# Last layer of a two-layer transformer kernel: top values turned before the first base products, next group's masks made in tile 5, base tile 0 opened with its x products

## The chip, the cores and the metric

The kernel runs on one core of a Trainium2 chip. The metric is the device time of one execution in microseconds (us), the median of several runs. Five engines work side by side, each with its own instruction queue, and meet only at semaphores: TensorE (PE, matrix products into PSUM; its weight loads are shown as PEld), VectorE (DVE), ScalarE (ACT), GpSimd (POOL) and SyncE (SP), which issues the DMAs here.

## The reference, cut to what matters

```python
x = x + tanh(g_xattn[0]) * L0_xattn(layernorm(x), ...)   # long convolution
x = x + tanh(g_ffn[0])   * L0_ffn(layernorm(x), ...)     # 8 experts and a shared one
x = x + tanh(g_xattn[1]) * L1_xattn(layernorm(x), ctx)   # attention, 16 heads
x = x + tanh(g_ffn[1])   * L1_ffn(layernorm(x), ...)     # the layer that is changed

# L1_ffn; B = 16 sequences, S = 128, D = 256, H = 704, 8 experts, rank 16
gate_logits = x @ gate_w.T
topw, sel = top_k(gate_logits, 2)
topw = softmax(topw, axis=1)              # over the sequence, not over the two
base_up, base_gate = x @ w_up.T, x @ w_gate.T
for e in range(8):
    c = sum(where(sel == e, topw, 0))
    lo_up   = 2 * (x @ up_A[e].T   @ up_B[e].T)
    lo_gate = 2 * (x @ gate_A[e].T @ gate_B[e].T)
    h_e = silu(base_up + lo_up) * (base_gate + lo_gate)
    ch = c * h_e
    mixed_h += ch
    lora_down += 2 * (ch @ down_A[e].T @ down_B[e].T)
out = mixed_h @ w_down.T + lora_down
```

## The kernel before

Four stages follow each other (convolution, experts, attention, and the last layer, about 620 to 894 us). Each takes the 16 sequences in G = 4 groups of 4 (512 tokens). The last layer works transposed: hidden units on partitions, the 512 tokens of a group along the free axis. The 704 hidden units are 6 tiles (j = 0 to 5, the last with 64 rows). Every product is done as three products of high and low halves (`three`, L1625, L1630), which ACT (high half, a copy) and DVE (low half, a subtraction) make for every operand.

Each token uses two experts. For its first expert a tile is computed as base products (`d_base`): 12 products of x with the weights (6 for up, 6 for gate), and 6 of the masked adapter values z. For its second, `d_delta` adds the difference of the adapters on top of the same PSUM bank (6 products). After each, ACT applies SiLU (L733) and DVE multiplies (L1202, L1206; after the second also the sum, L1210). ACT and DVE then split the two results (L741, L747; L1216, L1222) and `d_down` multiplies them down. `(j, 0)` is a tile's first expert and `(j, 1)` its second. TensorE runs base of tile j, delta of tile j-1, down of tile j-2.

At a change of group TensorE computes the adapter values of the next group (`d_adapters_in`, 12 products, into the PSUM areas U_[0] and G_[0]), then `d_down` of tiles 4 and 5, then `d_base(g+1, 0)`. DVE multiplies the adapter values with the masks (`d_split_z`, L1190, four of them, counted by `zm_ready`), ACT copies the high halves (L725), DVE makes the low halves (L1193, counted by `zL_ready`). Only when L1190 has read U_[0] and G_[0] may tile 0 be written there. DVE goes on with `d_mix` (L1228 to L1238) of the group that ends, and only then with the next group's first tile.

The masks come from the router: eleven small DVE steps find the two best experts (`top2_step`), TensorE turns the values to rows (`d_turn_tops`, L1653), DVE and ACT take the softmax over the sequence, SP stores the 16 rows and loads them back spread over all partitions (L387, L391, into `rb`), DVE compares them with each partition's expert number (`masks`, L1175, two instructions) and POOL subtracts the two masks (L488, `dMD`). `masks(n)` waits for the load; `d_split_z` waits for POOL.

The order on every engine is the order in which this code is written; nothing reorders it. `Steps.take(n)` weaves small steps between larger ones.

Of the kernel before, what the change touches and what calls it, by code (L numbers as in the profile page):

```python
# [107 lines left out]
def flamingo_kernel(nc, x, ctx_nat, ctx_half, ctx_t, ctx_one, filt, bias, gates, w0, wr, w1, gw, ramp_in, out):  # L108
    es = ExitStack()
    with es:  # L110
# [135 lines left out]
        for j in range(1, SJ):  # L246
# [40 lines left out]
        d_logits, lg_taken, tops_ready, tops_turned, tops_taken, topmax_ready, cexp_ready = (  # L287
            sem("d_logits"), sem("lg_taken"), sem("tops_ready"), sem("tops_turned"), sem("tops_taken"),
            sem("topmax_ready"), sem("cexp_ready"))
        rows_ready, rows_stored, rows_loaded = sem("rows_ready"), sem("rows_stored"), sem("rows_loaded")  # L290
        dM_ready, dMD_ready = sem("dM_ready"), sem("dMD_ready")
        z_psum, zm_ready, zH_ready, zL_ready = sem("z_psum"), sem("zm_ready"), sem("zH_ready"), sem("zL_ready")
        ev_ready, dsilu_ready, dscaled_ready, ch_ready, sum_ready = (
            sem("ev_ready"), sem("dsilu_ready"), sem("dscaled_ready"), sem("ch_ready"), sem("sum_ready"))
# [500 lines left out]
        def _(dve):  # L795
# [293 lines left out]
            def d_norm(lo, hi):  # L1089

                return norm_steps(hi - lo, lambda b: X[:, lo + b], pstat[:, lo:hi], pmv[:, lo:hi], pvar[:, lo:hi],
                                  ptmp[:, lo:hi], prs[:, lo:hi], pnb[:, lo:hi], None)
# [57 lines left out]
            def group_top2(n):  # L1150
                return Steps(lambda i: top2_step(i, n), N_TOP2)

            def rows_taken(n):

                dve.wait_ge(tops_turned, n + 1)
                if n:
                    dve.wait_ge(rows_stored, 16 * n)
                t_psum = TQ[0:4 * BG, P:2 * P] if n == 0 else U_[0][0:4 * BG, 0:P]
                nc.vector.tensor_copy(prow, t_psum).then_inc(tops_taken, 1)
# [6 lines left out]
            def rows_scale(n):  # L1166
                dve.wait_ge(cexp_ready, n + 1)
                link(nc.vector.reciprocal(mrcp, msum))
                nc.vector.tensor_scalar(prow[0:2 * BG], prow[0:2 * BG], mrcp, None, ALU.mult).then_inc(rows_ready, 1)

            def masks(n):

                dve.wait_ge(rows_loaded, 16 * (n + 1))
                for r in (2, 3):
                    nc.vector.tensor_scalar(rb[n % 2][:, r], rb[n % 2][:, r], expert_col, LORA_ALPHA,  # L1175
                                            ALU.is_equal, ALU.mult).then_inc(dM_ready, 1)

            def d_low_x(g):
                for k in range(DT):
                    dve.wait_ge(xH_ready, 2 * (G + g) + k + 1)  # L1180
                    nc.vector.tensor_tensor(xL[:, k], pxT[:, k], xH[:, k].bitcast(F32), ALU.subtract
                                            ).then_inc(xL_ready, 1)
# [13 lines left out]
            def d_rows(g, j, k):  # L1196

                i = at_ev[j, k]
                pr = TAIL if j == SJ - 1 else P
                dst = (dc1, dc2)[k]  # L1200
                dve.wait_ge(ev_ready, NE * g + i + 1)
                nc.vector.tensor_tensor(dscaled[0:pr, i % 2], G_[j % 2][0:pr], rb[g % 2][0:pr, k], ALU.mult  # L1202
                                        ).then_inc(dscaled_ready, 1)
                dve.wait_ge(dsilu_ready, NE * g + i + 1)
                dve.wait_ge(dscaled_ready, NE * g + i + 1)
                nc.vector.tensor_tensor(dst[0:pr, j % 2], dscaled[0:pr, i % 2], dsilu[0:pr, i % 2], ALU.mult  # L1206
                                        ).then_inc(ch_ready, 1)
                if k == 1:
                    dve.wait_ge(ch_ready, 1 + NE * g + i + 1)
                    nc.vector.tensor_tensor(dc2[0:pr, j % 2], dc2[0:pr, j % 2], dc1[0:pr, j % 2], ALU.add  # L1210
                                            ).then_inc(sum_ready, 1)

            def d_low_first(g, j):
                pr = TAIL if j == SJ - 1 else P
                dve.wait_ge(cH_ready, SJ * g + j + 1)
                nc.vector.tensor_tensor(dcL[0:pr, j % 2], dc1[0:pr, j % 2], dcH[0:pr, j % 2].bitcast(F32),  # L1216
                                        ALU.subtract).then_inc(cL_ready, 1)
# [40 lines left out]
            def d_tiles(g, more, top2):  # L1258
                norm = d_norm(B - BG, B) if g == 0 else Steps()
                for j in range(2, SJ):  # L1260
                    d_rows(g, j, 0)
                    top2.take(4)
                    if more and j == 4:
                        rows_scale(g + 1)
                    if more and j == 5:
                        norm.take_all()
                    d_rows(g, j - 1, 1)
                    top2.take_all()
                    if more and j == 3:
                        rows_taken(g + 1)  # L1270
                    if more and j == SJ - 1:
                        d_low_x(g + 1)
                    d_low_first(g, j)
                    if more and j == 3:
                        rows_shift(g + 1)
                    d_low_sum(g, j - 1)
                    if j >= 3:
                        norm.take(8)
                d_rows(g, SJ - 1, 1)
                d_low_sum(g, SJ - 1)  # L1280
                if more:
                    masks(g + 1)
                    dve.wait_ge(dn_ready, 1 + g)
                    d_split_z(g + 1)
                    dve.wait_ge(zL_ready, 4 * (g + 2))
                d_mix(g)
                top2 = group_top2(g + 2) if g + 2 < G else Steps()
                if more:
                    d_first(g + 1, top2)
                d_finish(g)  # L1290
                return top2
# [81 lines left out]
        def _(pe):  # L1373
# [273 lines left out]
            def d_turn_tops(n):  # L1647

                pe.wait_ge(tops_ready, n + 1)
                if n:  # L1650
                    pe.wait_ge(dsilu_ready, NE * (n - 1) + at_ev[2, 1] + 1)
                t_psum = TQ[0:4 * BG, P:2 * P] if n == 0 else U_[0][0:4 * BG, 0:P]
                nc.tensor.transpose(t_psum, ptop, ident[:]).then_inc(tops_turned, 1)  # L1653

            def d_adapters_in(g):

                pe.wait_ge(xL_ready, 2 * (G + g + 1))
                for r, dst in enumerate((U_[0], G_[0])):
                    a = [((w1H[:, r * D + k * P:r * D + (k + 1) * P], w1L[:, r * D + k * P:r * D + (k + 1) * P]),
                          (xH[:, k], xL[:, k])) for k in range(DT)]  # L1660
                    three(dst, a).then_inc(z_psum, 1)

            def d_base_in(g, j, part):

                pr = TAIL if j == SJ - 1 else P
                for at, dst, zr_ in ((0, U_[j % 2], 0), (2 * P, G_[j % 2], 2)):
                    if j >= 2 and zr_ == 2:
                        pe.wait_ge(dscaled_ready, NE * g + at_ev[j - 2, 1] + 1)
                    a = [(tuple(w[:, 0:pr] for w in w1_tile(j, at + k * P, P)), (xH[:, k], xL[:, k]))
                         for k in range(DT)]  # L1670
                    lora = [(tuple(w[:, 0:pr] for w in w1_tile(j, 4 * P + at // 2, P)), (dzH[:, zr_], dzL[:, zr_]))]
                    if part == "all":
                        mm = three(dst[0:pr], a + lora, skip=True)
                    elif part == "x":
                        mm = three(dst[0:pr], a, stop=False, skip=True)
                    else:
                        mm = three(dst[0:pr], lora, start=False, skip=True)
                return mm

            def d_base(g, j, part="all"):  # L1680
                if j >= 2:
                    pe.wait_ge(dsilu_ready, NE * g + at_ev[j - 2, 1] + 1)
                else:
                    pe.wait_ge(zm_ready, 4 * (g + 1))
                if j == 4 and g + 1 < G:
                    pe.wait_ge(tops_taken, g + 2)
                if j == 0:
                    pe.wait_ge(zL_ready, 4 * g + 2)
                d_base_in(g, j, part).then_inc(ev_ready, 1)

            def d_delta(g, j):

# [88 lines left out]
            pe.wait_ge(w1L_ready, W1K)  # L1781
            pe.wait_ge(shifted, 8 * G)
            d_adapters_in(0)
            d_base_in(0, 1, "x")
            pe.wait_ge(lg_taken, 1)
            d_turn_tops(0)
            d_turn(1)
            d_router(1)
            d_base(0, 0)
            d_base(0, 1, "z")  # L1790
            d_delta(0, 0)
            for g in range(G):
                d_tiles(g, g + 1 < G)
# [66 lines left out]
```

## Time and profile before

| | us |
|---|---|
| median of 3 runs | 894.28 |
| lowest, highest | 894.27, 897.79 |
| the profiled execution, its own time | 895.68 |
| its span, first to last instruction | 894.0 |
| PE busy | 794.3 (89%) |
| DVE busy | 611.6 (68%) |
| ACT busy | 325.1 (36%) |
| POOL busy | 164.1 (18%) |
| mean granted TensorE clock | 0.962 of full |

The page divides the span into 40 slices of 22.35 us; each digit is the busy share in tenths. The last layer is the last 12 slices:

```
PE   2887879699999999999998999987599999899995
DVE  5899999654466465457545888896368766677754
PEclk9999999899999999999999999978799999999997
```

TensorE is at nine tenths in most of it. The exceptions are the layer's opening (slices 28 and 29) and the end. PEclk is the clock granted to TensorE, in tenths of full speed; a 9 is full. It has two levels, 2.4 GHz (1.00) and 1.2 GHz (0.50). Times within the span are counted from its start, and all durations come from this one execution.

### The profile page before, as it was taken

To read this page: it belongs to the slowest core of one execution; us is meant where nothing else is said; L and a number is where in the kernel's file an instruction comes from. 1 tells how busy PE (TensorE), PEld (TensorE's weight loads), DVE (VectorE), ACT (ScalarE), POOL (GpSimd) and SP (SyncE) were. 2 spreads that over 40 slices of the span, in tenths; PEclk is the share of its full clock that TensorE was granted. 3 is DMA by queue.
4 is the path that set the end of the run, shared out by engine and by line. 5 is a ranking of instruction groups with operands and counts; after the bars stand their busy time and mean duration, and the time that the engine had idled before them with its cause. 6 is when DMAs were issued, how large, how long until landed. Compare 5 with 4: busy or idle time off the path is not lost. (4 is left out here: it accounts for less than half of the span.)

```text
span 894.0 us, 13688 instructions
## 1 busy us (share of the span) xinstructions
PE 794.3 (89%) x4708; PEld 638.3 (71%) x4708; DVE 611.6 (68%) x1231; ACT 325.1 (36%) x521; POOL 164.1 (18%) x176
## 2 busy tenths in 40 slices
PE   2887879699999999999998999987599999899995
PEld 2565657588878888888885666655477788787884
DVE  5899999654465466457545888896368766677754
ACT  2120212133433242342233677856235235343221
POOL 1899999500000000000000010100000000000000
PEclk9999999899999999999999999978799999999997
DMA  7221212000000000001001112110101001001000
GB/s 271 72 86 50 70 47 65 18 1 1 1 0 0 0 0 0 0 0 33 18 1 44 48 55 84 53 41 1 48 0 48 1 25 48 1 25 48 24 0 25
DMA packets 21147, 30.24 MB, mean 34 GB/s; under 512 B 3760, under 2 KB 16112, under 8 KB 20464
## 3 DMA queue, kind: packets, MB, share of 16 engines
q1 hardware_dynamic: 21104, 29.69, 10.1%
q8 instruction: 24, 0.39, 0.2%
q14 instruction: 19, 0.16, 0.1%
HBM read 27.55 MB, written 2.13 MB: 33 GB/s over the span
## 5 line engine op out<-in xcount | busy, mean ns | idle before, releaser
L1630 PE MATMUL bank<-R 128*128 128x512 f32 (+4 forms) x1104 | 230.9, 371 | 26.5 <-DVE R L1193 15.2
L1630 PEld LDWEIGHTS bank<-R 128*128 128x128 f32 (+2 forms) x1104 | 186.6, 191 | 68.3 <-issue 19.3
L1484 PE MATMUL bank<-R 128*128 128x512 f32 (+1 forms) x816 | 198.0, 392 | 1.9 <-issue 1.9
L1484 PEld LDWEIGHTS bank<-R 128*128 128x128 f32 (+1 forms) x816 | 146.7, 185 | 33.1 <-issue 2.2
L1009 DVE TENSOR_TENSOR A<-bank,A 128x512 f32<-128x512 f32 (+1 forms) x68 | 47.0, 692 | 119.9 <-PE bank L1484 119.9
L1497 PEld LDWEIGHTS bank<-R 128*128 128x128 f32 (+1 forms) x816 | 105.8, 190 | 10.8 <-issue 4.0
L1497 PE MATMUL bank<-R 128*128 128x256 f32 (+1 forms) x816 | 109.4, 284 | 2.5 <-DVE R L1020 2.1
L574 ACT ACTIVATE A<-bank 128x512 f32<-128x512 f32 (+1 forms) x68 | 40.6, 597 | 194.7 <-PE bank L1484 194.7
L1409 PE MATMUL bank<-A 128*128 128x256 f32 x128 | 44.1, 427 | 28.2 <-DVE A L857 19.2
L449 POOL TENSOR_TENSOR A<-A 128x256 f32<-128x256 f32 x64 | 64.2, 1002 | 10.6 <-DVE A L868 10.6
L1202 DVE TENSOR_TENSOR A<-bank,A 128x512 f32<-128x512 f32 (+1 forms) x48 | 32.9, 685 | 38.4 <-PE bank L1630 38.1
L857 DVE TENSOR_TENSOR A<-A 128x512 f32<-128x512 f32 x64 | 55.0, 861 | 0.4 <-ACT A L514 0.4
L1409 PEld LDWEIGHTS bank<-A 128*128 128x128 f32 x128 | 20.9, 196 | 47.4 <-DVE A L857 27.8
L478 POOL TENSOR_TENSOR R<-A,R 128x960 f32 x8 | 17.8, 2224 | 195.5 <-ACT R L627 195.5
L733 ACT ACTIVATE A<-bank 128x512 f32<-128x512 f32 (+1 forms) x48 | 28.6, 597 | 66.2 <-PE bank L1630 66.0
L1551 PE MATMUL bank<-ident,A 128*128 128x128 f32 x256 | 38.9, 301 | 13.7 <-ACT A L632 13.3
L868 DVE TENSOR_TENSOR A<-bank,A 128x512 f32<-128x512 f32 x64 | 43.5, 680 | 8.8 <-PE bank L1411 7.4
L1014 DVE TENSOR_TENSOR A<-A 128x512 f32<-128x512 f32 (+1 forms) x68 | 46.8, 688 | 3.1
L1551 PEld LDWEIGHTS bank<-ident,A 128*128 128x128 f32 x256 | 31.3, 154 | 23.8 <-ACT A L632 17.8
L1062 DVE TENSOR_REDUCE small<-bank 128x8 f32<-128x1024 f32 x32 | 39.0, 1220 | 13.3 <-PE bank L1541 13.1
L1020 DVE TENSOR_TENSOR R<-A,R 128x512 fp32r<-128x512 f32 (+1 forms) x68 | 46.2, 680 | 1.3 <-ACT R L583 1.2
L472 POOL MEMSET A<- 128x512 f32 x4 | 1.9, 524 | 229.3 <-DVE A L1014 229.3
(166 smaller groups left out, 1098.1 us busy)
## 6 DMA issues: line engine op xcount, KB each, us to landing
A<-in_w SPq DMA_DIRECT2D x17, 384.0 KB, 3.1
A<-rows_d SPq DMA_DIRECT2D x4, 1024.0 KB, 4.6
A<-in_w SPq DMA_DIRECT2D x8, 480.0 KB, 3.6
A<-in_ctx_one SPq DMA_DIRECT2D x8, 272.0 KB, 3.6
A<-in_ctx_half SPq DMA_DIRECT2D x8, 256.0 KB, 3.1
A<-in_ctx_nat SPq DMA_DIRECT2D x4, 512.0 KB, 3.6
A<-in_ctx_t SPq DMA_DIRECT2D x128, 16.0 KB, 2.0
out<-X SPq DMA_DIRECT2D x4, 512.0 KB, 2.9
```

The lines of the kernel that those rows point to most:

```text
L449: nc.gpsimd.tensor_tensor(zh[:, u], zr[:, u, :, 0:HALF, :], zr[:, u, :, HALF:, :], ALU.add).then_inc(zh_ready, 1)
L574: nc.scalar.activation(b_silu[0:pr, j % 2], G_[j % 2][0:pr], ACT.Silu).then_inc(silu_ready, 1)
L857: nc.vector.tensor_tensor(kv[:, u], vT[:, :, t0:t0 + I0].unsqueeze(3).to_broadcast([P, 8, I0, I0]), c.unsqueeze(2).to_broadcast([P, 8, I0, ...
L868: nc.vector.tensor_tensor(zr[:, u], yb[u].rearrange("p (q i j) -> p q i j", q=8, i=I0), c.unsqueeze(3).to_broadcast([P, 8, I0, I0]), ALU.m ...
L1009: nc.vector.tensor_tensor(b_scaled[0:pr, j % 2], U_[j % 2][0:pr], b_comb[0:pr, 0 if j < EJ else 1], ALU.mult).then_inc(scaled_ready, 1)
L1014: nc.vector.tensor_tensor(b_h[0:pr, j % 2], b_silu[0:pr, j % 2], b_scaled[0:pr, j % 2], ALU.mult).then_inc(h_ready, 1)
L1020: nc.vector.tensor_tensor(hL[0:pr, j % 2], b_h[0:pr, j % 2], hH[0:pr, j % 2].bitcast(F32), ALU.subtract).then_inc(hL_ready, 1)
L1409: nc.tensor.matmul(y[:, 0:n], diag, kv0, start=True, stop=False, skip_group_check=True)
L1484: mm = nc.tensor.matmul(dst[0:pr], wX[:, j, at + k * P:at + k * P + pr], mX[:, k], start=(n == 0), stop=(n == 5))
L1497: mm = nc.tensor.matmul(DN[:, b * D:(b + 1) * D], hX[0:pr, j % 2, b * P:(b + 1) * P], wX[0:pr, j, 4 * P:], start=(j == 0 and n == 0 and b ...
L1551: mm = nc.tensor.transpose(PTP[:, h * P:(h + 1) * P], E_[:, k % 2, h], ident[:])
L1630: mm = nc.tensor.matmul(dst, a, m, start=start and n == 0, stop=stop and n == len(prods) - 1, skip_group_check=skip)
```

## The change

There are three edits, all in the last layer.

1. On TensorE, `d_turn_tops(0)` moves ahead of the x products of tile 1 (`d_base_in(0, 1, "x")`) in the layer's opening.
2. On DVE, `masks(g + 1)` moves from behind tile 5 of group g into tile 5: behind the products of (5, 0), ahead of those of (4, 1). POOL's subtraction follows the masks by semaphore and so moves with them.
3. On TensorE, `d_base` of tile 0 waits for `zm_ready` only, issues its 12 x products, and waits for `zL_ready` ahead of the 6 z products. Before, both waits stood ahead of all 18.

```diff
@@ DVE, d_tiles
                     if more and j == 5:
                         norm.take_all()
+                        masks(g + 1)
                     d_rows(g, j - 1, 1)
@@
                 d_low_sum(g, SJ - 1)
                 if more:
-                    masks(g + 1)
                     dve.wait_ge(dn_ready, 1 + g)
                     d_split_z(g + 1)
@@ PE, d_turn_tops
                     pe.wait_ge(dsilu_ready, NE * (n - 1) + at_ev[2, 1] + 1)
+                else:
+                    pe.wait_ge(lg_taken, 1)
@@ PE, d_base
-            def d_base(g, j, part="all"):
+            def d_base(g, j):
@@
                 if j == 0:
+                    d_base_in(g, j, "x")
                     pe.wait_ge(zL_ready, 4 * g + 2)
-                d_base_in(g, j, part).then_inc(ev_ready, 1)
+                    d_base_in(g, j, "z").then_inc(ev_ready, 1)
+                else:
+                    d_base_in(g, j, "all").then_inc(ev_ready, 1)
@@ PE, the opening
             d_adapters_in(0)
+            d_turn_tops(0)
             d_base_in(0, 1, "x")
-            pe.wait_ge(lg_taken, 1)
-            d_turn_tops(0)
             d_turn(1)
             d_router(1)
             d_base(0, 0)
-            d_base(0, 1, "z")
+            pe.wait_ge(zL_ready, 2)
+            d_base_in(0, 1, "z").then_inc(ev_ready, 1)
```

The order on TensorE in the layer's opening, with what each instruction waits for (L1653 of before is L1655 of the change; L1598 turns the next group's x, L1643 is the router):

```order
 L1630 MATMUL bank<-R 128x512 [waits xL_ready,shifted,w1L_ready]
-L1630 MATMUL bank<-R 128x512 x23
-L1653 MATMUL bank<-ident,A 16x128 [waits tops_ready,lg_taken]
+L1630 MATMUL bank<-R 128x512 x11
+L1655 MATMUL bank<-ident,A 16x128 [waits lg_taken,tops_ready]
+L1630 MATMUL bank<-R 128x512 x12
 L1598 MATMUL bank<-ident,A 128x128 [waits vN_ready]
 L1598 MATMUL bank<-ident,A 128x128 x7
 L1643 MATMUL bank<-gw_sb,A 128x8 [waits xT_ready]
 L1643 MATMUL bank<-gw_sb,A 128x8 x7
-L1630 MATMUL bank<-R 128x512 [waits zL_ready,zm_ready]
-L1630 MATMUL bank<-R 128x512 x17
```

The turn stands behind 12 products in place of 24, and ahead of the 12 that were in front of it.

The order on DVE around the end of tile 5 of the first group (the same at the other two changes of group):

```order
+L1175 TENSOR_SCALAR A<-A,small 128x512 x2
 L1202 TENSOR_TENSOR A<-bank,A 128x512
 L1206 TENSOR_TENSOR A<-A 128x512
@@ -773,5 +774,4 @@
 L1210 TENSOR_TENSOR A<-A 64x512
 L1222 TENSOR_TENSOR R<-A,R 64x512
-L1175 TENSOR_SCALAR A<-A,small 128x512 x2
 L1190 TENSOR_TENSOR A<-bank,A 128x512 x4
 L1193 TENSOR_TENSOR R<-A,R 128x512 x4
```

The two mask instructions leave the place ahead of L1190 and stand ahead of (4, 1)'s L1202. Behind them are now that tile's L1202, L1206 and L1210, the next group's L1181, and the rest of tile 5.

The order on TensorE at the change to the second group:

```order
 L1630 MATMUL bank<-R 128x256 x12
-L1630 MATMUL bank<-R 128x512 [waits zL_ready,zm_ready]
-L1630 MATMUL bank<-R 128x512 x17
+L1630 MATMUL bank<-R 128x512 [waits zm_ready]
+L1630 MATMUL bank<-R 128x512 x11
+L1630 MATMUL bank<-R 128x512 [waits zL_ready]
+L1630 MATMUL bank<-R 128x512 x5
 L1598 MATMUL bank<-ident,A 128x128 [waits w_mixed,vN_ready]
```

Twelve of the 18 products of tile 0 no longer stand behind the wait for `zL_ready`.

## Rows read from the trace of the kernel before

**Rows 1.** The waits of TensorE: engine, line waited for, us, times, longest.

```profile
PE bank L1630 <- DVE R L1193: 15.2, 4, 9.6
```

**Rows 2.** Timeline, the layer's opening: start, us, instruction, [idle before it and its releaser].

```profile
624.84 7.25 PE L1630 MATMUL bank<-R 128*128 128x512 f32 x24 [1.87 <-DVE R L1181]
626.40 0.19 DVE L1148 TENSOR_REDUCE A<-A 128x4 f32<-128x32 f32 x1
...
631.92 0.27 PE L1653 MATMUL bank<-ident,A 128*16 128x128 f32 x1
...
640.03 0.88 DVE L1175 TENSOR_SCALAR A<-A,small 128x512 f32<-128x512 f32 x2 [5.96 <-DMA A<-rows_d]
...
642.29 2.49 DVE L1190 TENSOR_TENSOR A<-bank,A 128x512 f32<-128x512 f32 x4 [1.38 <-POOL A L488]
...
646.12 9.86 PE L1630 MATMUL bank<-R 128*128 128x512 f32 x30 [9.63 <-DVE R L1193]
```

**Rows 3.** Timeline, the second change of group (groups 1 to 2).

```profile
750.06 0.68 DVE L1202 TENSOR_TENSOR A<-bank,A 128x512 f32<-128x512 f32 x1
...
758.25 0.87 DVE L1175 TENSOR_SCALAR A<-A,small 128x512 f32<-128x512 f32 x2
759.20 1.27 POOL L488 TENSOR_TENSOR A<-A 128x512 f32<-128x512 f32 x1 [60.01 <-DVE A L1175]
760.56 2.48 DVE L1190 TENSOR_TENSOR A<-bank,A 128x512 f32<-128x512 f32 x4 [1.44 <-issue]
...
764.39 5.92 PE L1630 MATMUL bank<-R 128*128 128x512 f32 x18 [1.69 <-DVE R L1193]
765.49 0.69 DVE L1228 TENSOR_TENSOR A<-bank,A 128x512 f32<-128x512 f32 x1
...
770.36 0.69 DVE L1202 TENSOR_TENSOR A<-bank,A 128x512 f32<-128x512 f32 x1
...
770.95 4.34 PE L1630 MATMUL bank<-R 128*128 128x512 f32 x18
...
772.42 1.01 ACT L707 ACTIVATE A<-bank 128x1024 f32<-128x1024 f32 x1
```

**Rows 4.** Timeline, the first change of group.

```profile
692.11 8.80 PE L1630 MATMUL bank<-R 128*128 128x512 f32 x48 [0.50 <-DVE R L1181]
...
703.11 5.96 PE L1630 MATMUL bank<-R 128*128 128x512 f32 x18 [2.20 <-DVE R L1193]
```

**Rows 5.** Timeline, the third change of group.

```profile
813.43 1.29 DVE L1181 TENSOR_TENSOR R<-A,R 128x512 fp32r<-128x512 f32 x2
...
815.45 0.59 ACT L733 ACTIVATE A<-bank 64x512 f32<-64x512 f32 x1 [0.16 <-PE bank L1630]
...
825.65 12.87 PE L1630 MATMUL bank<-R 128*128 128x512 f32 x54 [1.71 <-DVE R L1193]
```

**Rows 6.** Stretches of TensorE: from:to, us, busy (x), granted clock, DMA share, GB/s.

```profile
634.00:635.00 1.00, 0.46 (x4) 1.00 0.01 3
...
652.00:652.50 0.50, 0.50 (x4) 0.98 0.00 0
...
703.00:703.50 0.50, 0.39 (x1) 0.72 0.00 0
...
706.50:707.00 0.50, 0.50 (x3) 0.87 0.00 0
```

**Rows 7.** The load of the spread rows: the second group change's issue, and all four loads' landing.

```profile
745.82 0.32 SPq L391 DMA_DIRECT2D A<-rows_d  x1
...
DMA to landing us min/median/max: 4.3/4.6/4.8
```

**Rows 8.** Timeline of DVE and POOL in the first stage.

```profile
153.97 0.72 POOL L449 TENSOR_TENSOR A<-A 128x256 f32<-128x256 f32 x1
154.09 0.65 DVE L943 TENSOR_TENSOR small<-small,ramp 128x32 f32<-128x32 f32 x1
...
161.22 0.19 DVE L943 TENSOR_TENSOR small<-small,ramp 128x32 f32<-128x32 f32 x1
```

## The prediction, made before the changed kernel ran

> **What bounds the kernel now.** I read the busy table first: TensorE is busy 89% of the span, so what its queue waits for is the candidate. In the view of waits, one row of the last layer stands out: the products of L1630 wait 15.2 us in four waits for L1193, the low halves of z [rows 1]. The timeline shows the four: 9.63 us at the opening [rows 2], 2.20, 1.69 and 1.71 us at the three changes of group [rows 3 to 5]. The wait is not the whole price. The 18 products behind the wait at 764.39 take 5.92 us, the 18 at 770.95 take 4.34 us [rows 3]. The granted clock says why: 1.00 until the restart at 703.11, half speed (1.2 GHz) from about then, full again (2.4 GHz) from about 706.6 [rows 4, 6]. So a change of group costs its wait and 5.92 - 4.34 = 1.6 us of slow products. Inside the groups TensorE hardly waits; whatever is saved at these four places moves all that follows.
>
> **Edit 1, the turn.** At 624.84 TensorE starts 24 products and only then turns the top values, at 631.92 [rows 2]. The values were ready at 626.6 (626.40 + 0.19), so the turn waits for its place in the queue alone. It now stands 12 products earlier. A product at full clock takes (4.34 - 0.39)/17 = 0.23 us, with 0.39 us as the part of a product that overlaps nothing (an estimate: the 4.34 us row holds 18 of them); those skipped run behind the clock's rise. The turn comes 12 x 0.23 = 2.8 us earlier, at about 629.1, still behind 626.6. From there the chain is a pure one: softmax, store, load, masks, POOL, L1190. DVE stands idle 5.96 us before the masks for the load alone, and 1.38 us for POOL [rows 2]. The whole chain moves by 2.8 us, and the displaced products fill time in which TensorE would idle anyway.
>
> **Edit 3 at the opening.** TensorE restarts at 646.12, when the second L1193 is done. L1190 ended at 642.29 + 2.49 = 644.78 [rows 2]. With x first it restarts 1.3 us sooner, and its 12 x products outlast the making of the low halves. Together 2.8 + 1.3 = 4.1 us. One cost is unknown: after this restart the clock stays low until 652.0 (5.9 us), while at 703.11 it stays low for 3.5 us [rows 6]. If the low clock lasts 3.5 us in the new opening it gains 1.2 us more (half of 2.4); if it lasts 3.5 us longer than before it gains 1.7 less. I take it unchanged.
>
> **Edit 2, the masks.** It takes three things out of DVE's path to L1190 and puts two into tile 5. Before, from the masks' start to L1190's is 760.56 - 758.25 = 2.31 us [rows 3]: masks, POOL, hand-over. In tile 5 the masks cost 0.87 us. Behind them on DVE are L1202, L1206 and L1210 of (4, 1), then L1181, for which the next group's adapter products wait.
>
> The second cost is POOL. Its 1.27 us subtraction used to run while DVE waited; now it runs beside DVE. In the first stage, a small DVE operation with both inputs in SBUF takes 0.65 us when it is issued under a POOL operation, and 0.19 us alone; it ends just when POOL does (154.74 against 154.69) [rows 8]. L1202 has one input in PSUM and I take it as free; L1206 has both in SBUF, would start 0.7 us behind the masks, and POOL ends 1.35 us behind them: 0.6 us more. So DVE is 0.87 + 0.6 = 1.47 us late from L1206 on. The bounds are 0.87 (POOL hinders nothing) and 0.87 + 1.27 = 2.1 us (POOL holds up L1202 too).
>
> The Trainium skill, "SBUF — State Buffer", section "Who interferes with whom", says the same in general: a VectorE instruction with two SBUF inputs contends with a GpSimd instruction that reads SBUF, one with a single SBUF input does not, and the loser blocks fully. By it the sum is the one I take; a reader of the removed wait alone, without it, would forecast 1.8 us more over three groups.
>
> What DVE's lateness costs TensorE depends on the slack of L1181. At the first change there is none: the adapter products already waited 0.50 us for it [rows 4], so TensorE gets the full 1.47 us and its wait becomes 1.97 us. At the third, L1181 ends at 814.72 and the products before the adapters end at about 815.3 (the ACT row at 815.45, less a product's overlap) [rows 5]: slack 0.55, cost 0.9 us. The second looks the same.
>
> Then the gain. DVE reaches L1190 2.31 - 1.47 = 0.84 us earlier than before, at 759.7, ends it at 762.2; TensorE ended its down products at 764.39 - 1.69 = 762.70 and will now at 763.6. So there is no wait in front of tile 0 any more. The second L1193 follows L1190's end by 1.3 us (763.5): the split of tile 0 is hardly needed here, edit 2 alone nearly does it. A queue that runs on also loses the overlap of about 0.2 us that a stop exposes. Per change of group: wait removed, plus 0.2, plus 1.6 of clock, less the lateness:
> - first: 2.20 + 0.2 + 1.6 - 1.47 = 2.5 us
> - second: 1.69 + 0.2 + 1.6 - 0.9 = 2.6 us
> - third: 1.71 + 0.2 + 1.6 - 0.9 = 2.6 us
>
> **What is late next.** The router of group g + 2 waits for L707, which hangs on DVE's chain: it ended at 773.43 [rows 3] and gains only the 0.84 us of DVE, to 772.6. TensorE would come to it at 775.3 - 2.6 = 772.7. So the second change keeps 2.5 us, the first about the same. DVE's mixing (L1228 from 765.49 to the next L1202 at 770.36) [rows 3] also gains only 0.84 us, and tile 0's products will be ready some 1.8 us ahead of it; the 18 products of tile 1 cover that.
>
> The clock is the other thing. At the first change the adapters' wait becomes 1.97 us. Waits of 2.20, 1.69 and 1.71 us were each followed by the low clock; the stretch with the router's 1.48 us wait kept 1.00 [rows 6]. 1.97 is on the wrong side: I count 1.6 us against it and keep 0.9 us there. At the other two the wait is 0.9 us, on the right side.
>
> The load must have landed when DVE reaches the masks. At the second change it is issued at 745.82 and lands 4.3 to 4.8 us later, 750.1 to 750.6, while DVE is there at 750.06 [rows 3, 7]: 0 to 0.5 us of wait, mostly within the slack; I take 0. At the other changes the store before the load was quicker.
>
> **Sum.** 4.1 + 0.9 + 2.5 + 2.6 = 10.1 us. The profiled execution took 895.68 us, of which 894.0 are its span; it becomes 885.6. It lies 1.40 us above the median, so the median goes from 894.28 to 884.2 us.
>
> **Rivals.**
> - *POOL hinders nothing and the clock holds.* Then DVE is late by 0.87 us only, each change keeps 0.6 us more, and the first loses nothing to the clock: 4.1 + 3.1 + 3.1 + 3.2 = 13.5, giving 880.8 us. For it: L1202's class of operation is unhindered. Against: rows 8. Chance 0.15.
> - *The adapters' wait brings the low clock at every change.* Three waits of 0.9 to 2.0 us, each followed by 1.6 us of slow products: 4.1 + 0.9 + 0.9 + 1.0 = 6.9, giving 887.4 us. Against: 1.48 us did nothing. Chance 0.13.
> - *DVE's mixing takes the wait's place.* If tile 0's late start on DVE and ACT is not covered by tile 1, each change gives what DVE's chain gains, 0.84 us: 4.1 + 2.5 = 6.6, giving 887.7 us. For it: DVE was just in time before. Chance 0.13.
> - *It gives nothing at the changes and little at the opening*, because the chain behind the turn is not what ends the wait: within 0.5% of before. Against: the load as releaser in rows 2. Chance 0.05.
> - *Slower: the masks block DVE for a load that lands late.* In tile 5 everything that feeds TensorE is queued behind them. A load that is L us late makes TensorE L us later at each change and brings the clock's 1.6 us with it; without both, the gains add up to 4.1 + 2.5 + 2.6 + 2.6 = 11.8 us. It decides where 3 x (L + 1.6) is more than 11.8, from L = 2.3 us. With L = 5, a load of twice its length, 19.8 - 11.8 = 8.0 us slower, 902.3 us. Four loads land within 0.5 us of each other. Chance 0.02.
>
> The forecast itself has 0.52.
>
> **Range.** It reaches from 880.4, just past the rival at 880.8, to 888.2, past those at 887.4 and 887.7. Outside are the last two rivals (0.07), and of the others what the opening's -1.2 to +1.7 us carries over the ends, about 0.13. No-change is about 0.5% here, 4.5 us, so faster means below 889.8: chances 0.93 faster, 0.05 the same, 0.02 slower.
>
> **What the changed profile would show.** The turn near 629, the masks near 637.3, the restart of TensorE near 642. L1175 directly behind (5, 0)'s L1206, with POOL's L488 beside L1202, and the L1206 behind it near 1.3 us in place of 0.69. No wait for L1193 or L1190 at the changes of group and full clock in tile 0; a wait of 2.0 us for L1181 at the first change with half clock behind it, and of about 0.9 us at the others. I am wrong if waits appear before tile 2 of the new groups, if L1175 waits for the DMA, or if L1206 keeps 0.69 us.

## The result and the profile after

| | before | changed |
|---|---|---|
| median, us (4 runs each) | 895.03 | 884.62 |
| lowest, highest | 894.27, 897.79 | 884.33, 886.95 |
| ratio, 95% interval | | 0.988 (0.986 to 0.989) |
| profiled execution, its span | 895.68, 894.0 | 884.61, 882.9 |

The change is 1.2% faster, 10.4 us by the medians. The forecast was 884.2 us, with a range of 880.4 to 888.2; it was counted from 894.28 us, the median of the three runs then on record.

Of TensorE's waits in the last layer, L1193's 15.2 us [rows 1] are gone. The longest waits of these products (L1630) in the changed kernel:

```profile
PE bank L1630 <- DVE A L1190: 5.0, 1, 5.0
PE bank L1630 <- DVE R L1238: 4.9, 1, 4.9
PE bank L1630 <- DVE R L1181: 4.4, 3, 1.9
```

The wait for L1190 is what is left of the opening's 9.63 us. The one for L1238, at the end, was there before with the same 4.9 us. Of the three for L1181, the opening's 1.86 us is old too; those at the changes of group, 1.82 and 0.76 us, stand in place of 0.50 and none.

To see where the time went, the layer is cut at rows that both kernels have: the first L1181 (low half of x), and for each group the L1202 of (5, 0), the first of the group's with 64 rows (the mark, below). The end of the last piece is that of the last L1244, the final sum (890.60 us before, 879.53 after). Before:

```profile
623.40 1.28 DVE L1181 TENSOR_TENSOR R<-A,R 128x512 fp32r<-128x512 f32 x2
...
686.11 0.68 DVE L1202 TENSOR_TENSOR A<-bank,A 64x512 f32<-64x512 f32 x1 [0.62 <-PE bank L1630]
...
748.66 0.68 DVE L1202 TENSOR_TENSOR A<-bank,A 64x512 f32<-64x512 f32 x1 [2.12 <-PE bank L1630]
```

After:

```profile
624.48 1.28 DVE L1181 TENSOR_TENSOR R<-A,R 128x512 fp32r<-128x512 f32 x2
...
682.15 0.68 DVE L1202 TENSOR_TENSOR A<-bank,A 64x512 f32<-64x512 f32 x1 [0.62 <-PE bank L1630]
...
742.18 0.68 DVE L1202 TENSOR_TENSOR A<-bank,A 64x512 f32<-64x512 f32 x1 [2.12 <-PE bank L1630]
...
801.15 0.68 DVE L1202 TENSOR_TENSOR A<-bank,A 64x512 f32<-64x512 f32 x1 [2.12 <-PE bank L1630]
```

The opening, 686.11 - 623.40 = 62.71 us, became 57.67; the first change of group, 748.66 - 686.11 = 62.55, became 60.03. The same differences for every kernel of this study, each from its own profile:

| us | opening | change 1 | change 2 | change 3 | end | sum |
|---|---|---|---|---|---|---|
| before | 62.71 | 62.55 | 61.25 | 58.51 | 22.18 | 267.20 |
| the change | 57.67 | 60.03 | 58.97 | 56.20 | 22.18 | 255.05 |
| the change, again | 57.84 | 60.07 | 59.03 | 56.20 | 22.17 | 255.31 |
| edit 1 alone | 60.11 | 62.50 | 61.28 | 58.49 | 22.18 | 264.56 |
| edit 2 alone | 62.85 | 60.03 | 59.38 | 56.20 | 22.18 | 260.64 |
| edit 3 alone | 62.14 | 61.29 | 61.12 | 55.61 | 22.19 | 262.35 |
| edits 1, 2 | 59.48 | 60.04 | 59.87 | 56.18 | 22.19 | 257.76 |
| edits 1, 3 | 59.00 | 61.28 | 61.15 | 55.63 | 22.17 | 259.23 |
| POOL later | 59.09 | 60.05 | 61.05 | 55.71 | 22.18 | 258.08 |
| masks late | 58.92 | 61.42 | 58.63 | 55.16 | 22.19 | 256.32 |
| unread products | 58.76 | 60.06 | 59.01 | 56.20 | 20.94 | 254.97 |
| masks and router late | 58.97 | 59.06 | 57.96 | 55.17 | 22.19 | 253.35 |
| the same, no edit 3 | 59.38 | 61.59 | 58.70 | 55.91 | 22.19 | 257.77 |
| all together | 56.22 | 59.04 | 57.96 | 55.16 | 20.93 | 249.31 |

The changes and the end repeat within 0.1 us wherever the same thing happens. The opening does not: with the same code in it, it took 57.67, 57.84, 58.92, 58.97 and 59.09 us (the change twice, masks late, masks and router late, POOL later), and the changed kernel's first profile is the shortest of these. The gain of 12.15 us is 5.04 in the opening and 2.52, 2.28 and 2.31 at the changes; some 1.4 us of the 5.04 is what another execution may not have. The span gained 1.1 us less, since this execution reached the layer later (624.48 against 623.40), in code that is the same. That part varies from 621.5 to 626.7 over the profiles. So for the changes and the end the table is finer than the medians; differences of an us in the opening or in the sum are not to be read.

The opening's timeline after, to be laid beside [rows 2]:

```profile
625.90 4.78 PE L1630 MATMUL bank<-R 128*128 128x512 f32 x12 [1.86 <-DVE R L1181]
...
630.52 0.27 PE L1655 MATMUL bank<-ident,A 128*16 128x128 f32 x1
...
638.37 0.88 DVE L1175 TENSOR_SCALAR A<-A,small 128x512 f32<-128x512 f32 x2 [5.69 <-DMA A<-rows_d]
...
643.17 7.00 PE L1630 MATMUL bank<-R 128*128 128x512 f32 x22 [4.96 <-DVE A L1190]
```

Counted from L1181, the turn moved from 8.52 to 6.04 us, the masks from 16.63 to 13.89, the restart of TensorE from 22.72 to 18.69: 4.0 us sooner. The last 1.0 us of the opening is the clock: low until 652.02 before, 5.9 us behind the restart, and here until 646.8, 3.7 us behind it. In the other four profiles with this opening it stayed low for 3.3 to 5.9 us behind the restart. The stretch in which it rose (beside [rows 6]):

```profile
646.00:647.00 1.00, 1.00 (x4) 0.59 0.00 0
647.00:648.00 1.00, 1.00 (x6) 1.00 0.00 0
```

The second change of group after, beside [rows 3]:

```profile
743.57 0.87 DVE L1175 TENSOR_SCALAR A<-A,small 128x512 f32<-128x512 f32 x2
...
744.37 0.68 DVE L1202 TENSOR_TENSOR A<-bank,A 128x512 f32<-128x512 f32 x1
744.52 1.30 POOL L488 TENSOR_TENSOR A<-A 128x512 f32<-128x512 f32 x1 [57.67 <-DVE A L1175]
745.15 1.22 DVE L1206 TENSOR_TENSOR A<-A 128x512 f32<-128x512 f32 x1
...
748.44 13.12 PE L1630 MATMUL bank<-R 128*128 128x512 f32 x66 [0.76 <-DVE R L1181]
...
764.65 1.01 ACT L707 ACTIVATE A<-bank 128x1024 f32<-128x1024 f32 x1
...
766.37 1.85 PE L1643 MATMUL bank<-gw_sb,A 128*128 128x8 f32 x16
```

L1206 behind the masks ends at 746.37 and takes 1.22 us, beside POOL's subtraction, which ends at 745.82. TensorE then runs 66 products through: 12 adapter products, the downs of tiles 4 and 5 and tile 0, with no stop where it waited 1.69 us. The first change is the same with a wait of 1.82 us:

```profile
689.47 13.11 PE L1630 MATMUL bank<-R 128*128 128x512 f32 x66 [1.82 <-DVE R L1181]
```

66 products take 13.11 us here and 13.12 there, so neither is slow; the granted clock behind the 1.82 us wait is 1.00 throughout:

```profile
689.50:690.00 0.50, 0.50 (x2) 1.00 0.00 0
690.50:691.00 0.50, 0.50 (x4) 1.00 0.00 0
692.50:693.00 0.50, 0.50 (x4) 1.00 0.00 0
```

### The profile page after: what moved, and what is told of

Its sections match the earlier page's. It is cut to its first block, busy times and chain, and to the rows that moved or that the text cites. A ratio compares the mean times of both kernels' runs of the same rounds, so it can differ in the third digit from the quotient of the medians.

```text
span 882.9 us, 13668 instructions
## 1 busy us (share of the span) xinstructions
PE 790.2 (90%) x4692; PEld 638.1 (72%) x4708; DVE 613.5 (69%) x1231; ACT 325.4 (37%) x521; POOL 163.9 (19%) x176
## 4 chain that ended last, share of the span: by engine, by line
PE 67%; DVE 18%; issue 7%; POOL 3%; ACT 3%; DMA 1%; DVEq 0%; SPq 0%; POOLq 0%; ACTq 0%
PE bank L1630 23%; PE bank L1484 20%; PE bank L1497 11%; DVE small L1062 2%; PE bank L1551 2%; DVE A L868 2%; DVE A L857 2%; PE bank L1537 2%; POOL A L449 2%; DVE A L1072 2%; PE bank L1409 2%; ACT A L632 1%; PE bank L1411 1%; PE bank L1410 1%; PE bank L1562 1%
## 5 line engine op out<-in xcount | busy, mean ns | idle before, releaser
L1630 PE MATMUL bank<-R 128*128 128x512 f32 (+4 forms) x1104 | 225.9, 365 | 19.1 <-DVE A L1190 5.0
L1630 PEld LDWEIGHTS bank<-R 128*128 128x128 f32 (+2 forms) x1104 | 182.3, 188 | 60.1 <-issue 6.0
L1202 DVE TENSOR_TENSOR A<-bank,A 128x512 f32<-128x512 f32 (+1 forms) x48 | 32.9, 685 | 33.0 <-PE bank L1630 32.8
L733 ACT ACTIVATE A<-bank 128x512 f32<-128x512 f32 (+1 forms) x48 | 28.6, 596 | 58.4 <-PE bank L1630 58.3
```

What stands on the lines that cost most here:

```text
L1630: mm = nc.tensor.matmul(dst, a, m, start=start and n == 0, stop=stop and n == len(prods) - 1, skip_group_check=skip)
```

## The experiments

A ratio is the kernel's median over that of before, with its 95% interval; the differences within the layer are from the table above. Five kernels hold parts of the change; that with edits 1 and 2 comes further down.

**Edit 1 alone**: `d_turn_tops(0)` ahead of `d_base_in(0, 1, "x")`, nothing else.

> The kernel before with edit 1 alone (the turn of the top values ahead of tile 1's x products). My account: the restart of TensorE in the opening comes 2.7 us sooner, the three changes of group keep their waits of 1.7 to 2.2 us and the low clock behind them; 2.7 us faster, give or take 1.2 for the length of the low clock, so some 891.5. Rival (the gain of the change lies in the opening alone): 10 us faster or more.

Ratio 0.997 (0.995 to 0.999); opening 2.60 us less, changes unmoved (the waits of 2.21, 1.69 and 1.70 us are there). The turn gives the opening 2.6 us in these profiles, and nothing else, as expected.

**Edit 2 alone**: `masks(g + 1)` in tile 5.

> The kernel before with edit 2 alone (masks in tile 5). My account: the opening as before; at the changes no or hardly any wait before tile 0 and no low clock there, but waits of 1.8, 0.8 and 0.8 us before the adapter products; L1206 behind the masks 1.2 us in place of 0.69. 7.1 us faster (2.5, 2.3, 2.3), so about 887.2. Rival (edit 3 is what removes the waits at the changes): no more than 2 us faster.

Ratio 0.9945 (0.993 to 0.996); changes 2.52, 1.87 and 2.31 us less, where 2.5, 2.3 and 2.3 were expected. Edit 2 alone gives what the whole change gives at the changes of group, but for 0.4 us at the second. There, the masks waited for the load:

```profile
745.96 0.68 DVE L1206 TENSOR_TENSOR A<-A 64x512 f32<-64x512 f32 x1
746.97 0.88 DVE L1175 TENSOR_SCALAR A<-A,small 128x512 f32<-128x512 f32 x2 [0.33 <-DMA A<-rows_d]
```

**Edit 3 alone**: x products of tile 0 ahead of the wait for `zL_ready`.

> The kernel before with edit 3 alone (tile 0's x products ahead of the wait for the low halves of z). The waits before tile 0 shrink by 1.3 us to 0.9, 0.4 and 0.4, which by the waits seen so far are too short to bring the low clock, so 1.6 us more at each. Where the router of the next group but one waits for ACT (L707, unmoved) the gain is cut to 1.6 us. Opening 1.3, changes 1.6, 1.6 and 2.8: 7.3 us faster, about 887. Rival (as my prediction put it, the split is hardly needed at the changes): 1.3 to 2 us faster.

Ratio 0.995 (0.993 to 0.997); 4.85 us less in the layer, where 7.3 was expected. The third change is right (2.90). At the first the wait shrank to 0.92 us as expected, but the clock fell all the same:

```profile
702.02 5.99 PE L1630 MATMUL bank<-R 128*128 128x512 f32 x18 [0.92 <-DVE A L1190]
```

The granted clock of three stretches there:

```profile
702.00:702.50 0.50, 0.48 (x2) 1.00 0.00 0
702.50:703.00 0.50, 0.50 (x4) 0.71 0.00 0
703.00:703.50 0.50, 0.50 (x3) 0.50 0.00 0
```

So only 1.26 us came, where 1.6 was expected. At the second change tile 0 ran at full clock, the router met L707 (0.53 us), and the clock fell at 774.4, right behind its small products: 0.13 us is left of the 1.6. The opening gave 0.57 us in place of 1.3: TensorE restarted 2.54 us behind L1190's start in place of 3.83, but the rest of the opening came out longer.

**Edits 1 and 3**, the masks left in their old place.

> The change without edit 2: the masks stay behind tile 5. If edits 2 and 3 remove the same wait, this is about as fast as the whole change: opening 4.1, changes 1.6, 1.6 and 2.8, so 10.1 us faster than before, 884.2. Rival (edit 2 carries the changes of group): 5 us faster, about 889.5, with waits of 1.5 us and more before tile 0.

Ratio 0.991 (0.987 to 0.994), between the two accounts: 7.97 us less. The waits before tile 0 were 0.91, 0.41 and 0.41 us, not the rival's 1.5. Changes as in edit 3 alone (1.27, 0.10, 2.88), with the same two falls of the clock.

**The whole change again**, beside the next three.

> The whole change again, on the chip of the three beside it: 0.988 of before. In the last layer alone, from the first low half of x (L1181) to the end, 255 us as in its first profile. If the low clock appears at the first change of group this time, behind its wait of 1.8 us, 1.6 us more.

Ratio 0.985 (0.982 to 0.988); 255.31 us, and no low clock behind the 1.82 us wait.

**Edits 1 and 2**:

```diff
                 if j == 0:
-                    d_base_in(g, j, "x")
                     pe.wait_ge(zL_ready, 4 * g + 2)
-                    d_base_in(g, j, "z").then_inc(ev_ready, 1)
+                    d_base_in(g, j, "all").then_inc(ev_ready, 1)
```

> The change without edit 3 (tile 0 waits for the low halves of z before all of its 18 products). My account: the changes of group as in the whole change, since the low halves are there in time; only the opening restarts 1.3 us later. The last layer takes 256.4 us in place of 255.05. Rival (edit 3 carries the changes as well): waits of 1 us and more before tile 0, 3 us or more slower than the whole change.

Ratio 0.989 (0.985 to 0.992). Changes 60.04 and 56.18 against 60.03 and 56.20: edit 3 adds nothing there. The second lost 0.9 us to the load again, which was 0.76 us late this time. The adapters' wait there grew to 1.60 us, and the 66 products behind it are still at full clock:

```profile
745.13 0.88 DVE L1175 TENSOR_SCALAR A<-A,small 128x512 f32<-128x512 f32 x2 [0.76 <-DMA A<-rows_d]
...
750.01 13.14 PE L1630 MATMUL bank<-R 128*128 128x512 f32 x66 [1.60 <-DVE R L1181]
```

The opening restarts at 19.96 us against 18.69, 1.3 us later, as expected. It is 1.8 us longer than the change's 57.67, but only 0.4 us longer than the longest opening with the same code as the change. The layer took 257.76 us, 1.4 more than expected.

**POOL later**: the whole change, with one wait more on POOL.

```diff
                 if n:
                     pool.wait_ge(zm_ready, 4 * n)
+                    pool.wait_ge(xL_ready, 2 * (G + n + 1))
```

> The whole change, but POOL's subtraction of the masks waits until L1181 (the low halves of the next x) is done. If POOL and DVE block each other over their SBUF reads, L1206 behind the masks falls back from 1.22 to 0.69 us, a later DVE operation with two SBUF inputs is stretched instead, the adapters' waits shrink from 1.82, 0.76, 0.76 to 1.3, 0.2, 0.2, and the last layer takes 1.6 us less (253.4). Rival (the stretched L1206 has another cause, or the adapters wait for something else): 255.

Ratio 0.984 (0.981 to 0.988). The mechanism showed, the gain did not. L1206 is back at 0.69 us (lines behind the new one count one more in this file: L1206 is L1207, L1222 is L1223) and the first wait at 1.30 us, but the DVE operation that is now issued under POOL's is stretched more than L1206 was, from 0.68 to 1.80 us:

```profile
687.42 1.59 POOL L489 TENSOR_TENSOR A<-A 128x512 f32<-128x512 f32 x1 [48.70 <-DVE R L1182]
687.76 1.80 DVE L1223 TENSOR_TENSOR R<-A,R 128x512 fp32r<-128x512 f32 x1
```

The third change gained 0.49 us. At the second the load was 0.56 us late, and L1222 was stretched by 1.1 us, where L1206 had been by 0.5. So the router's input (L707) came 1.2 us later than in the whole change: TensorE waited 0.24 us for it, the clock fell at 768.4, and the change took 61.05 us, 2.1 more than in the whole change. At the first change the same wait of 0.24 us was followed by no fall. The layer took 258.08 us, where 253.4 was expected.

**Masks late**: the whole change, with the masks behind (5, 1)'s products.

```diff
                     if more and j == 5:
                         norm.take_all()
-                        masks(g + 1)
@@
                 d_rows(g, SJ - 1, 1)
+                if more:
+                    masks(g + 1)
                 d_low_sum(g, SJ - 1)
```

> The whole change, but the masks stand behind (5, 1)'s products, ahead of the last low half L1222, where DVE waits 0.7 us for ACT. L1181 is on time: adapters wait 0.5, 0 and 0. Masks, POOL and L1190 then end at about the time TensorE is free, and with edit 3 the 12 x products cover the making of the low halves. By my account the last layer takes 2 us less (253). Rival (the masks' chain is late again): a wait for L1190 of 0.5 us or more before tile 0 and no gain, or the low clock behind it and 1 to 3 us lost.

Ratio 0.984 (0.981 to 0.987). Changes 2 and 3 gained 0.34 and 1.04 us; change 1 lost 1.39. The layer took 256.32 us, where 253 was expected. Tile 0 did not wait, so the masks' chain is in time, although POOL's subtraction is now the one that is stretched, behind L1222:

```profile
692.94 0.68 DVE L1222 TENSOR_TENSOR R<-A,R 64x512 fp32r<-64x512 f32 x1
693.09 1.67 POOL L488 TENSOR_TENSOR A<-A 128x512 f32<-128x512 f32 x1 [52.97 <-DVE A L1175]
```

The trouble is later: TensorE waits 0.54 us for the router's input, and the 18 products behind the small ones take 4.59 us where they took 3.07 in the whole change:

```profile
707.66 1.95 PE L1644 MATMUL bank<-gw_sb,A 128*128 128x8 f32 x16 [0.54 <-ACT A L707]
...
709.47 4.59 PE L1631 MATMUL bank<-R 128*128 128x256 f32 x18
```

At the second change the router waited too, and the clock stayed:

```profile
767.84 1.95 PE L1644 MATMUL bank<-gw_sb,A 128*128 128x8 f32 x16 [0.39 <-ACT A L707]
```

The ratios of the change, POOL later and masks late in this comparison (0.985, 0.984, 0.984) do not tell the three kernels apart; the stretches between the marks do.

**Masks and router late**: as before, and the router behind the adapter products.

```diff
                     d_base(g + 1, 1)
-                    if g + 2 < G:
-                        d_router(g + 2)
                 d_adapt(g)
+                if g + 2 < G:
+                    d_router(g + 2)
```

> The version with the masks behind (5, 1)'s products, and the router of the next group but one behind the last group's adapter products on TensorE in place of ahead of them. My account of that version's lost gain at the first change is that TensorE, 1.3 us earlier, met the router's input (L707) too soon, waited 0.54 us and fell to half clock. With the router later both go: from (5, 0) of one group to (5, 0) of the next 59.5 us at the first change and 58.2 at the second (whole change: 60.0 and 59.0), 55.2 at the third. Rival (the low clock there has another cause): 61.4 at the first again.

Ratio 0.983 (0.980 to 0.986); 59.06, 57.96, 55.17. The router does not wait, and the clock falls at no change; the only wait there is the 0.50 us for L1181 at the first. That is what the account of the router said. Against before the changes are 3.5, 3.3 and 3.3 us shorter.

**The same without edit 3.**

> The version with late masks and late router, without edit 3. If edit 3 is what the late masks need, tile 0 waits again, by some 1 us at each change (the low halves of z are there 1.3 us after L1190), and if the clock falls behind those waits 1.6 us more: 60.1 to 61.7, 59 to 60.6, 56.2 to 57.8 at the three changes (59.1, 58.0 and 55.2 with edit 3), and the opening restarts 1.3 us later. Rival (edit 3 is covered here too): the changes as with it.

Ratio 0.990 (0.987 to 0.993); 61.59, 58.70, 55.91: 2.5, 0.7 and 0.7 us longer than with edit 3. Tile 0 waits 1.20, 0.71 and 0.71 us, and only behind the first does the clock fall:

```profile
698.86 5.96 PE L1631 MATMUL bank<-R 128*128 128x512 f32 x18 [1.20 <-DVE R L1193]
...
759.20 4.33 PE L1631 MATMUL bank<-R 128*128 128x512 f32 x18 [0.71 <-DVE R L1193]
```

**Unread products**: the whole change, and products into PSUM that is free at the time and read by no one.

```diff
             d_router(1)
+            pe.wait_ge(tops_taken, 1)
+            pe.wait_ge(c_done, B)
+            for _ in range(14):
+                nc.tensor.matmul(DN[:, 0:512], w1H[:, 0:P], xH[:, 0], start=True, stop=True, ...)
             d_base(0, 0)
@@ behind the last d_down
+                if not more:
+                    for _ in range(19):
+                        nc.tensor.matmul(bank[0][:, 0:512], w1H[:, 0:P], xH[:, 0], start=True, stop=True, ...)
```

> The whole change, and products that nothing reads put into two waits of TensorE: 14 behind the router in the opening (it waits 5 us there and then runs 3.3 to 3.7 us at half clock), and 19 ahead of the last adapter products (a wait of 4.9 us, behind which the clock is at half for 12 products in 2.93 us). If the clock follows what TensorE did before, both stretches are at full clock: opening 1.7 us less, end 1.0 us less; the last layer takes 252.5 us in place of 255.1. Rival (the clock falls at these places whatever TensorE does, or the added products overrun the waits): 255 or more.

Ratio 0.985 (0.982 to 0.988). The end gained 1.24 us: 12 products in 1.70 us, which took 2.93. The opening, 58.76 us, gained nothing that stands out of its spread. The 14 ended too early, TensorE rested 2.76 us, the clock fell at 642.9, and the 30 products behind took 9.94 us (8.81 in the change):

```profile
637.40 3.45 PE L1801 MATMUL bank<-R 128*128 128x512 f32 x14
643.61 9.94 PE L1631 MATMUL bank<-R 128*128 128x512 f32 x30 [2.76 <-DVE A L1191]
```

**All together**: late masks, late router, 20 unread products in the opening and 19 at the end.

> Masks behind (5, 1)'s products, router behind the adapter products, and the unread products in both waits, now 20 in the opening (14 ended 2.8 us before TensorE was wanted, and the clock fell in that rest). Changes as in the version with the late router (59.1, 58.0, 55.2), end 1.2 us less, opening 1.7 us less if the clock holds: the last layer in 250.5 us (253.35 without the fills, 255.1 in the whole change). Rival (the opening's clock falls all the same, or the 20 overrun): 252 to 253.

878.46 us median, ratio to before 0.980 (0.978 to 0.983), against 0.988 and 0.985 for the change in its two comparisons: the fastest kernel here. The layer takes 249.31 us, 1.2 less than forecast. The wait behind the 20 products is 1.51 us, the clock holds, and the 30 products take 7.11 us, where they took 8.60 to 9.84 in the five profiles of the change's opening:

```profile
635.75 4.81 PE L1802 MATMUL bank<-R 128*128 128x512 f32 x20
642.07 7.11 PE L1632 MATMUL bank<-R 128*128 128x512 f32 x30 [1.51 <-DVE A L1191]
```

## Why the prediction was right, and where it was not

**The turn** (2.8 us forecast): right. Its queue place was all that held it; 2.48 us at the turn, 2.74 at the masks, 2.60 in the opening when made alone. Other profiles put the turn 5.6 to 6.7 us behind L1181 with the edit and 8.5 to 9.6 without, so no single pair gives it finer than about 1 us.

**Edit 3 at the opening** (1.3 us): right. The restart came 4.0 us sooner with both; and in every kernel with edit 3 TensorE restarts 2.54 us behind L1190's start, in every one without it 3.83. The clock's unknown, bounded at 1.2 us gained to 1.7 lost, came out at 1.0 gained in the change's first profile. That was luck of the execution: the change's opening took up to 1.4 us longer in others.

**The masks and POOL** (0.87 + 0.6 us of lateness on DVE): right. L1206 takes 1.22 us at all three changes, forecast 1.3; L1181 starts 1.31 us later behind the mark, forecast 1.47; and the adapters' waits are 1.82, 0.76 and 0.76 us, forecast 1.97, 0.9 and 0.9 (at the third the view names L733, which ended 0.01 us behind L1181). The slack of 0.55 us that the prediction read at the third change comes out, too: 1.31 - 0.76. That DVE and POOL hold each other up is shown from both sides: with the masks late, L1222 was issued first and POOL's subtraction took 1.67 us in place of 1.27; with POOL ahead, L1206 or L1222 was stretched. The rival in which POOL hinders nothing is out.

**"On the wrong side"** is the step that failed. I counted 1.6 us for a fall of the clock behind a wait of 1.97 us at the first change. It was 1.82 us and the clock stayed at 1.00, in each of the five profiled kernels with this wait (the change twice, edit 2, edits 1 and 2, the unread products). The change gained 2.52 us there, where 0.9 was forecast; 2.5 was the working without that term, though with the measured 1.32 us of lateness that working gives 2.7. The same term was wrong in my expectation for edit 3, in the other direction: 0.92 us was followed by the low clock. A wait's length alone does not sort them: 0.92 and 1.20 fell, 1.82 held. The place does, with the length. The prediction priced a wait ahead of the adapter products by waits ahead of tile 0. Ahead of the adapter products, at the changes of group in the 14 profiles, there are 26 waits of 0.24 to 1.82 us, and the clock fell behind none. Ahead of tile 0, behind the down products, it fell behind the nine waits of 0.91 to 2.21 us and behind none of the six of 0.40 to 0.71. The falls at the router's small products, behind waits of 0.24 to 0.54 us, are a third case, and there the same waits of 0.24 and 0.39 us also passed without one. What it is in the work around a wait that decides stays open.

**The second and third changes** (2.5 and 2.6 us): 2.28 and 2.31. The lateness was 0.76 us in place of 0.9, so the rest, 0.2 for the overlap and 1.6 for the clock, gave 2.28 - 1.69 + 0.76 = 1.35 us and is 0.45 too large. The clock's part is right: 18 products of tile 0 take 4.33 us at full clock even behind a wait of 0.71 us, against 5.92, so 1.59; and edit 3 alone, which cut the third wait from 1.71 to 0.40 us, gained 2.90 = 1.31 + 1.59. It is the 0.2 for the overlap that is mis-sized, and its counterpart that is missing. Giving back a wait of 0.71 us ahead of tile 0 (the last version without edit 3) cost 0.74 us, so only 0.03 us of overlap. The adapters' new wait of 0.76 us cost more than itself: without it (masks and router late) the third change takes 55.17 us in place of 56.20, 1.03 less. With these the third change adds up: 1.71 + 0.03 + 1.59 - 1.03 = 2.30 us, measured 2.31. This is worked out from pairs of kernels; no run isolates it, and at the first change the same sum, 2.9, is 0.4 too large.

**The load's margin** (0 to 0.5 us at the second change): real, and larger than taken. Of the six profiled kernels with the masks in tile 5 the load was in time in three (the change twice, unread products) and 0.33, 0.56 and 0.76 us late in three (edit 2, POOL later, edits 1 and 2). In the first three it was issued 1.4 us behind the store, in the others 3.0 to 3.4 us behind it, as before (745.82). So the change's profiles had the good case, and 0.33 and 0.76 us late cost the second change 0.4 and 0.9 us: nothing of it went into slack. The prediction's own sign, L1175 waiting for the DMA, appeared in half of the cases. The rival of the late load was right in that TensorE pays for it, wrong in that it loses the clock: it held behind 1.19 and 1.60 us.

**Edit 3 at the changes** ("edit 2 alone nearly does it"): shown, by edits 1 and 2 against the whole. The three edits overlap: alone they save 2.64, 6.56 and 4.85 us, 14.05 in sum, and together 12.15. At the changes of group alone edit 2 saves 6.70 us and edit 3 4.29, and both together 7.11.

**The rivals.** DVE's mixing does not take the wait's place: it starts 1.2 us sooner (15.64 us behind the mark at the second change, 16.83 before) and the products of tile 1 cover it. The rival in which the adapters' wait brings the low clock at every change is out. The router's input was not as close as worked out (772.6 against 772.7): L707 came 1.3 us sooner, where 0.84 was forecast, and ended at 765.66, 0.7 us before the router's products started at 766.37. It became the bound in the first kernels that went further.

The total was right partly by luck. The forecast for the layer was 10.1 us and 12.15 were measured: 1.6 more at the first change, 0.9 more in the opening, 0.5 less at the other two. Against it stand the 1.1 us by which the part ahead of the layer was slower in that execution, and the medians, which fell by 10.4 us, hold openings of other lengths.

## What to carry to other kernels

When a wait before a stretch of work is removed, count the slow products behind it as well, but treat the clock as a term with both outcomes: here it was lost behind 0.9 us in one place of the order and kept through 1.8 us in another, so a price read at one place does not carry to the next. An operation that is moved into another's cover brings its followers with it: here POOL's subtraction, harmless in an empty stretch, cost 0.5 us beside a DVE operation with two SBUF inputs. And work that comes sooner may meet the next input too soon, so look at the order behind it: from the version with late masks, moving the router behind the adapter products turned a loss of 1.4 us into a gain of 1.0.

## What the runs showed of the hardware

- A TensorE wait of 4.9 us at the end, filled with 19 products nobody reads for 4.62 us, left the next products at full clock: 12 in 1.70 us in place of 2.93. In the opening 4.81 us of such products in a wait of 6.3 us did the same: 30 in 7.11 us, in place of 8.60 to 9.84. Filled for 3.45 of 6.2 us, it helped nothing.
- At a change of group the clock fell during 16 products of 8 columns, or up to 1.1 us behind them, in four kernels (edit 3 alone, edits 1 and 3, POOL later, masks late), with waits of only 0.24 to 0.54 us ahead of them. Behind such waits of 0.24 us (POOL later, first change) and 0.39 us (masks late, second change) it stayed full, and at the changed kernel's own changes of group, without a wait, too. In the opening the same products stand behind 1.11 or 1.48 us; there the clock fell during them in five of the 14 profiles (2.07 to 2.67 us for the 16, the change's two among them) and not in nine (1.95 us).
- A wait of TensorE can cost more than its length: 0.76 us ahead of the adapter products cost 1.03 us, 0.71 us ahead of tile 0 cost 0.74.
- A DVE operation with two SBUF inputs and a POOL operation that reads SBUF hold each other up by order of issue: POOL 1.27 to 1.59 or 1.67 us behind DVE, DVE 0.68 to 1.22 or 1.80 us behind POOL.
- The store of the 16 rows, up to the load's issue, took 1.4 us in some profiles and 3.0 to 3.4 in others, in the same place of the same code.
